# Attention stage of a two-layer block: the turns, score products and small steps of one tile in another sequence on three engines

## The reference

```python
x = x + _L0_xattn_ref(_layernorm(x), ctx_1024, ctx_1024, Wq, bq, Wk, bk, Wv, bv, Wo, bo, temperature)
x = x + _L0_ffn_ref(_layernorm(x), w1, b1, w2, b2)           # quantised, 512 -> 2048 -> 512
x = x + _L1_xattn_ref(_layernorm(x), ctx_1024, ctx_1024, ...)  # scores without softmax, so linear
x = x + _L1_ffn_ref(_layernorm(x), ...)                       # three products and tanh
...
    Q = (query @ Wq.T + bq).reshape(B, Nq, H, D).transpose(0, 2, 1, 3)
    K = (key @ Wk.T + bk).reshape(B, Nkv, H, D).transpose(0, 2, 1, 3)
    V = (value @ Wv.T + bv).reshape(B, Nkv, H, D).transpose(0, 2, 1, 3)
    scores = jnp.einsum('bhqd,bhkd->bhqk', Q, K) * SCALE
    scores = scores / temperature
    attn = jax.nn.softmax(scores, axis=-1)
    out = jnp.einsum('bhqk,bhkd->bhqd', attn, V)
    out = out.transpose(0, 2, 1, 3).reshape(B, Nq, C)
    return out @ Wo.T + bo
```

## Time and profile before

| | us |
|---|---|
| median of three runs (1825.88 to 1826.61) | 1826.12 |
| the profiled execution, its own time | 1827.0 |
| span of the profiled execution | 1825.2 |
| PE busy in the span | 1748.5 (96%) |
| DVE busy | 1563.2 (86%) |
| ACT busy | 1223.4 (67%) |
| POOL busy | 982.1 (54%) |

### The profile page before, as it was taken

How to read it: one execution, slowest core, us unless ns; L and a number is a source line. 1 busy time by engine, 2 the same in 40 slices (tenths; PEclk the granted TensorE clock), 3 DMA queues, 4 the chain that set the end, 5 groups by cost and what they waited for, 6 DMA issues and landing times.

```text
span 1825.2 us, 29834 instructions
## 1 busy us (share of the span) xinstructions
PE 1748.5 (96%) x9082; PEld 1304.0 (71%) x9162; DVE 1563.2 (86%) x3584; ACT 1223.4 (67%) x3374; POOL 982.1 (54%) x1079
## 2 busy tenths in 40 slices
PE   8898799999999999999889999889999999999997
PEld 7786688888888888888644444457777776767775
DVE  6866789999999999988679888878888988888885
ACT  4575899999999999999533333356656655665543
POOL 2544466666666666666500000156766767767665
PEclk9999999999999999999989999999999999999999
DMA  8666445554455545544379999054445445445311
GB/s 306 201 211 186 105 124 142 153 156 139 139 153 154 146 137 157 154 117 121 93 240 389 407 395 385 26 219 171 167 151 197 161 154 197 153 163 170 124 58 41
DMA packets 153902, 322.08 MB, mean 176 GB/s; under 512 B 47376, under 2 KB 55568, under 8 KB 136080
## 3 DMA queue, kind: packets, MB, share of 16 engines
q1 hardware_dynamic: 153280, 319.38, 53.7%
q10 hardware_dynamic: 464, 0.79, 0.2%
HBM read 163.86 MB, written 105.91 MB: 148 GB/s over the span
## 4 chain that ended last, share of the span: by engine, by line
PE 45%; DVE 2%; issue 1%; ACT 1%; POOL 1%; POOLq 0%; DVEq 0%; ACTq 0%
PE f_pair L1575 12%; PE f_pair L1628 11%; PE f_pair L68 6%; PE f_pair L70 6%; PE f_pair L69 6%; PE f_pair L1615 3%; PE f_pair L1586 1%; ACT f_hf L1696 0%; DVE w L1801 0%; DVE f_st L1833 0%; POOL f_rs L1992 0%; ACT f_room L1671 0%; POOL f_ring L2020 0%; ACT f_hf L1688 0%; DVE f_x2Tl L1821 0%
## 5 line engine op out<-in xcount | busy, mean ns | idle before, releaser
L1320 POOL TENSOR_TENSOR a_pr<-a_pr,a_rcp 128x512 f32<-128x512 f32 x256 | 266.4, 1041 | 262.8 <-DVE a_rcp L1162 262.5
L1070 ACT ACTIVATE a_pr<-a_s,a_nmax 128x128 f32<-128x128 f32 x1024 | 365.4, 385 | 26.9 <-DVE a_nmax L1155 25.1
L1070 ACT ACTIVATION_READ_ACCUMULATOR a_pr<-a_s,a_nmax 128x1 f32 x1024 | 229.3, 224 | 0.0
L1575 PE MATMUL f_pair<-f_room,w 128*128 128x512 bf16 x999 | 225.2, 382 | 2.6 <-ACT f_room L1684 1.3
L1992 POOL TENSOR_TENSOR f_rs<-f_rs,f_half 128x1 f32<-128x1 f32 x128 | 121.2, 947 | 179.2 <-DVE f_rs L1839 179.2
L1793 DVE CUSTOM_DVE_ANT_0 f_hf<-f_pair,nb,sh 128x512 f32<-128x512 f32 x244 | 172.7, 748 | 29.8 <-PE f_pair L1575 29.5
L1575 PEld LDWEIGHTS f_pair<-f_room,w 128*128 128x128 bf16 x1024 | 99.6, 99 | 116.9 <-issue 3.8
L1155 DVE TENSOR_REDUCE a_nmax<-a_s 128x4 f32<-128x512 f32 x256 | 172.0, 672 | 9.6 <-PE a_s L961 7.5
L1170 DVE TENSOR_TENSOR a_pTl<-a_pt,a_pTh 128x512 fp32r<-128x512 f32 x256 | 168.5, 679 | 12.7 <-ACT a_pTh L1082 12.7
L973 PE MATMUL a_pt<-ident,a_pr 128*128 128x128 f32 x1024 | 160.7, 280 | 16.1 <-DVE a_pTl L1170 8.1
L1082 ACT ACTIVATE a_pTh<-a_pt 128x512 fp32r<-128x512 f32 x256 | 151.7, 628 | 4.5 <-PE a_pt L973 4.5
(11 more groups left out here) (443 smaller groups left out, 5091.7 us busy)
## 6 DMA issues: line engine op xcount, KB each, us to landing
hidden<-f_hf SPq DMA_DIRECT2D x57, 1024.0 KB, 8.6
f_hf<-hidden SPq DMA_DIRECT2D x57, 1024.0 KB, 4.8
xr<-x SPq DMA_DIRECT2D x96, 256.0 KB, 3.1
xb<-x SPq DMA_DIRECT2D x16, 1024.0 KB, 5.4
x<-xr SPq DMA_DIRECT2D x64, 256.0 KB, 2.3
ctxh<-bqreph SPq DMA_DIRECT2D x126, 128.0 KB, 2.4
f_room<-x SPq DMA_DIRECT2D x15, 1024.0 KB, 10.3
ctxh<-bqreph SPq DMA_DIRECT2D x128, 64.0 KB, 2.0
```

Of the source, the lines that this page charges most:

```text
L1070: last = e.activation(pr[:, t, j, :], s_bank[t][:, j * P:j * P + P], ACT.Exp, bias=nmax[kk % 2][:, t, j:j + 1], accum_out=sums[kk % 2][:, ...
L1320: e.tensor_tensor(p, p, rcp[kk % 2][:, t, :].unsqueeze(2).to_broadcast([P, 4, KEYS]), ALU.mult).then_inc(*e_pn)
L1575: last = e.matmul(h_bank[(PAIRS * u + i) % 3][:, q, :], w1[:, k, f * P:f * P + P], xT[u % 2][:, k, :], start=k == 0, stop=k == KC - 1)
```

## The change

Nothing is added or taken away. In a step of the middle:

- PE: `scores(3)` goes ahead of `pt(2)`, and `xt` ahead of `pt(3)`.
- ACT: the second `vlow` copy goes behind `exp(2)`, and `xhi` behind `phi(2)` and `phi(3)`.
- DVE: `smax(2)` goes ahead of `rc(1)`, and `xlo` behind `rc(2)` and the two `plo`.

In the very first step `xhi` and `xlo` stood at the later place already; PE, `vlow` and `smax` change there too. POOL and SP keep their lists.

```diff
@@ PE
                 scores(b, kk, 2)
                 values(b, kk)
+                scores(b, kk, 3)
                 pt(b, kk, 2)
-                scores(b, kk, 3)
+                xt(b, kk)
                 pt(b, kk, 3)
-                xt(b, kk)
                 out(b, kk)
@@ ACT
-            def vlow(b, kk):
+            def vlow(b, kk, i):
...
-                for i in range(2):
-                    e_pv.wait_ge(e, 2 * u + i)
-                    e_vs.wait_ge(e, 2 * (u - 1) + i)
-                    e.activation(vl[64 * i:64 * i + 64, :], v_bank[i][64 - 64 * i:128 - 64 * i, :], ACT.Copy).then_inc(*e_vl)
+                e_pv.wait_ge(e, 2 * u + i)
+                e_vs.wait_ge(e, 2 * (u - 1) + i)
+                e.activation(vl[64 * i:64 * i + 64, :], v_bank[i][64 - 64 * i:128 - 64 * i, :], ACT.Copy).then_inc(*e_vl)
...
                 qhi(b, kk)
-                vlow(b, kk)
+                vlow(b, kk, 0)
                 exp(b, kk, 2)
-                if not opening:
-                    xhi(b, kk)
+                vlow(b, kk, 1)
                 phi(b, kk, 2)
                 phi(b, kk, 3)
-                if opening:
-                    xhi(b, kk)
+                xhi(b, kk)
                 chi(b, kk)
                 exp(b, kk, 3)
@@ DVE
+                smax(b, kk, 2)
                 rc(b, kk, 1)
-                smax(b, kk, 2)
                 qlo(b, kk)
                 vsum(b, kk, 0)
                 smax(b, kk, 3)
                 vsum(b, kk, 1)
-                if not opening:
-                    xlo(b, kk)
                 rc(b, kk, 2)
                 plo(b, kk, 2)
                 plo(b, kk, 3)
-                if opening:
-                    xlo(b, kk)
+                xlo(b, kk)
                 x1_stats(b, kk)
```

## The result

The changed kernel takes 1834.16 us (median; 1831.69 to 1837.0 over six runs), the kernel before 1826.0 in the same comparison (1822.53 to 1827.38, six runs). The ratio is 1.0047 [1.0037, 1.0058]: **slower by 0.47%**, where 1817.1 and a gain were forecast, and outside the range. The profiled execution took 1834.35, with a span of 1832.5 against 1825.2 before.

What follows compares the result with a forecast made beforehand. A ring through ScalarE, VectorE and TensorE (11.24 us a step) was taken as the bound, TensorE needing 11.02. Gains 8.0 - 1.8 + 1.3 + 0.6 + 0.9 = 9.0 us gave 1817.1 us, range 1811.5 to 1823.5.

Steps and rivals of the forecast that it cites:

- The ring of 11.24: Middle steps: a chain through ScalarE, VectorE and TensorE sets the 11.24 us period; the change makes it 10.94.
- floor of 11.02: Middle steps: TensorE's own work takes 11.02 us and becomes the bound after the change.
- The idle 0.33: ScalarE waits 0.33 us ahead of the second `vlow` copy for TensorE to fill its bank; the change removes this.
- first rival: `prob(3)` or `plo` still holds TensorE in most steps; gain 0.08 a step, 4.2 us in all, 1822; chance 0.20.
- The lower bound: Whole kernel: VectorE's wait ahead of `vsum(1)`, shown by no row, halves the gain, giving 1822 us.
- Steps of unequal gain: Of four middle steps, two with `norm` gain 0.21 each, two with `stats` 0.11 and 0.07; 8.0 us over 53 steps.
- The batch boundary: Twelve steps around changes of batch: queries come late, SyncE's unchanged list sets the pace, minus 1.8 us of gain.
- The ends: Opening four steps gain 1.3 us; closing gains 0.6 over four steps and 0.9 over the last three.
- The third: VectorE becomes the bound if its stall passes 0.3; 26 `stats` steps lose 0.16 each, `norm` gains nothing; 1830; chance 0.06.
- The second: Steps at a change of batch wait longer by all the others gained, clock or next part takes the rest; 1826; chance 0.10.
- The fourth: TensorE's clock falls because twelve transposes stand in a row; 1.0 us a step, 64 in all, 1890; chance 0.02.
- the cover: The 0.7 us by which `xlo` was to release the next `queries` (6.4) ahead of their start (7.1).

Runs made afterwards that it cites:

- The last two experiments: Second `vlow` copy put between two halves of tile 2's exponentials: in the changed kernel 1817.27 us, in the kernel before, nothing else changed, 1819.43 us.
- the kernel with the halves: Changed kernel with the second `vlow` copy between the exponentials of heads 0, 1 and heads 2, 3 of tile 2: 1817.27 us, ratio 0.9956.

## Why the prediction was wrong

**What bounds the kernel: right.** The ring of 11.24 over a floor of 11.02 was there. One reading in it was off: "11.24 - 0.33 = 10.91" for ScalarE's own list leaves in the idle 0.34 ahead of `exp(0)`. Without both it is 10.57, so ScalarE already waited for VectorE before, and its 0.33 was worth something only as far as VectorE came earlier too. The last two experiments take the 0.33 out and arrive at 11.05, with the turns at 0.60.

**ScalarE: nearly right.** The idle 0.33 went. `exp(2)` started at 704.41 - 702.59 = 1.82 (forecast 1.80) and the second copy at 3.36 (forecast 3.18). `exp(2)` takes 1.54 of the engine and not 1.38: the copy starts 0.24 behind the last accumulator read (705.95 - 705.71) where the next instruction stood 0.09 behind it before. `exp(3)` starts at 5.94 (forecast 5.76) and still ends 0.34 ahead of `rc(3)`, so this alone would have left ScalarE time.

**VectorE: the step that failed**, in "`rc(2)` comes at 3.83 + 0.61 = 4.44" and "4.44 + 2.89 = 7.33". Measured are 4.78 and 7.80. The 0.47 between them, part by part:

| | forecast | measured | miss |
|---|---|---|---|
| `vsum(1)`, by ScalarE's late copy | 3.83 | 4.05 | 0.22 |
| `vsum(1)` to `rc(2)` | 0.61 | 0.73 | 0.12 |
| `rc(2)` to `rc(3)` (`plo` stands 0.20 behind `rc(2)`, not 0.09) | 2.89 | 3.02 | 0.13 |

None is large. But the whole margin was 7.63 - 7.33 = 0.30, and the three together turn a gain of 0.30 into a loss of 0.17. With 7.80 in the ring, 10.94 becomes 11.40. The prediction had called a small error in either of two paths the reason for its first rival, and looked at 0.08 as the margin to TensorE's floor; the margin that mattered was the 0.30 over the state before, all of it on the path that now had a wait in it whose price no row showed. The lower bound ("the gain halves") was too narrow for such a term: it should have reached over zero.

**Steps of unequal gain.** The forecast of the `stats` steps failed by the same term: `exp(2)` at 715.98 - 713.99 = 1.99 (forecast 2.03), but `vsum(1)` at 4.21 and `rc(3)` at 7.96, and the step 725.56 - 713.99 = 11.57. They are the longer ones, as forecast. **The batch boundary** was counted as 1.8 of the gain lost. Its mechanism, SyncE's list sets the pace there, held with the sign turned: 3.4 of the loss were swallowed. **The ends**: the opening gained 0.5 of a forecast 1.3. In the closing the four steps forecast to gain 0.6 took 10.77 to 10.93 where they had taken 10.74 to 10.81; the 1.4 gained behind them came from the one step with a lower clock, which no part of the forecast had in it.

**The rivals.** The third had the mechanism and the sign: `vsum(1)` waits for the late copy, everything behind it on VectorE too. Its stall was 0.60 and 0.35, past its point of 0.3. It had the loss in the `stats` steps alone and no gain in the others, and so priced 1830 and not 1834; and with 0.06 it had far too small a chance, since the own text put the stall at 0.45 and the point from which it decides at 0.3, so its condition was already met by the numbers of the forecast. The first rival had a piece of it, a ring that closes elsewhere and stays above TensorE's floor, but expected half the gain. The second showed only with its sign turned, at the changes of batch. The fourth was not: the clock stood at 1.00 in both stretches, with twelve transposes in a row. The `xt` was held only slightly, and no `queries` were held by `xlo` in the change, though the cover was 0.23 wide in the `norm` step above (`xlo` ends at 709.46, the `queries` start at 709.69) and not 0.7.

## What to carry to other kernels

Where two engines' lists close a ring together, idle time taken out of one is worth only what the other's list gives up too: before a move, write down for both when each handed-over item comes, and take as margin the distance to the state before, not to the next floor. A producer that is moved behind 1.5 us of other work moves everything that stands behind its consumer; if it had to wait only 0.33, put just enough work ahead of it (here half the exponentials) to cover that wait. Work that is moved into a gap delays what stands behind it by as much as it is longer than the gap, so look at the step with the narrowest gap, and at what another engine takes from the end of that list: 1.11 us of work gained in the steps with a gap of 0.60 and lost in those with 0.35.

## What the runs showed of the hardware

The second sum, on partitions 64 to 127, costs VectorE more than its own place. Behind `vsum(0)`, on partitions 0 to 63, the next instruction starts 0.60 later (705.36 - 704.76, same step). Behind `vsum(1)` the next instruction starts 0.73 later (707.37 - 706.64) where instructions of the same length in the same list follow each other in 0.60 (709.38 - 708.78 for `xlo` and `x1_stats`), that is only when the sum has ended. When this next instruction is the reciprocal, which reads no PSUM, the first one behind it that does is held as well: `plo` stands 707.57 - 707.37 = 0.20 behind it, and 0.09 before. With the reciprocal ahead of the sum there was one such hold (0.73), with `xlo` directly behind it one too (0.72). The Trainium skill, VectorE: DVE Perf Modes, section Two Vector instructions with no wait between them, says that an instruction is held until all earlier ones have finished if it starts to read or write, in SBUF or in PSUM, at another group of 32 partitions than the last one that did so there; the trace agrees, in both places.

ScalarE's copies of 64 partitions behave alike in the rows, at 0.60 to 0.62 each: `exp(2)` follows the first 704.41 - 703.79 = 0.62 behind its start, though ScalarE's other copies of the same 512 columns are followed by the next after 0.48 (708.01 - 707.53 for `xhi`), and the second copy stood 0.24 behind an accumulator read of 0.21. Both copies read at one half of the partitions and write at the other. In the kernel with the halves the second copy interrupts the exponentials, and the `norm` steps still ran at TensorE's pace. Whether start partitions are the reason on ScalarE too was not tried.
